# Attention output kept by channel and divided on GpSimd, in an FFN, attention, FFN block on one core

## The reference

```python
x = x + 0.5 * _L0_ffn_ref(_layernorm(x), w_gate, w_up, w_down)
x = x + _L0_attn_ref(_layernorm(x), Wq, Wk, Wv, Wo)
x = x + 0.5 * _L0_ffn_ref(_layernorm(x), w_gate, w_up, w_down)

def _L0_attn_ref(x, Wq, Wk, Wv, Wo):
    ...
    logits = jnp.where(causal_mask, neg, einsum('bhqd,bhkd->bhqk', q, k) * scale)
    out = einsum('bhqk,bhkd->bhqd', softmax(logits), v)
    return out.transpose(0, 2, 1, 3).reshape(B, T, D) @ Wo.T
```

## Time and profile before

| | us |
|---|---|
| median of 3 runs (2227.59 to 2228.46) | 2228.16 |
| the profiled execution | 2228.96 |
| its span, first to last instruction | 2227.2 |
| first feed-forward network, 40 to 460 | 420 |
| products for queries, keys, values, 460 to 690 | 230 |
| attention, 690 to about 1687 | 997 |
| output product, to about 1756 | 69 |
| second feed-forward network, to the end | 471 |

### The profile page before, as it was taken

How to read it: one execution, slowest core, us unless ns; L and a number is a source line. 1 busy time by engine, 2 the same in 40 slices (tenths; PEclk the granted TensorE clock), 3 DMA queues, 4 the chain that set the end, 5 groups by cost and what they waited for, 6 DMA issues and landing times. The chain is left out here.

```text
span 2227.2 us, 50129 instructions
## 1 busy us (share of the span) xinstructions
PE 2087.8 (94%) x13960; PEld 1374.4 (62%) x13960; DVE 1923.9 (86%) x4807; ACT 1313.3 (59%) x2413; POOL 1005.3 (45%) x1671
## 2 busy tenths in 40 slices
PE   4799999997998999999999999999998799999998
PEld 3688888886883333333333333333336788888887
DVE  6799999996987888888888888988863699999996
ACT  3455555543762777777677777777784344555553
POOL 4788888873654011111011111101110288888884
PEclk7899999998996999999999999999998899999998
DMA  6000000002689665545665546665403100000000
GB/s 210 1 1 0 0 0 0 0 1 71 229 234 181 76 78 72 72 65 70 77 78 66 71 63 77 78 78 67 55 12 122 35 16 19 19 19 19 19 19 25
DMA packets 163272, 133.33 MB, mean 60 GB/s; under 512 B 78432, under 2 KB 138208, under 8 KB 163040
## 3 DMA queue, kind: packets, MB, share of 16 engines
q1 hardware_dynamic: 163104, 131.25, 32.8%
HBM read 79.82 MB, written 51.38 MB: 59 GB/s over the span
## 5 line engine op out<-in xcount | busy, mean ns | idle before, releaser
L1413 POOL TENSOR_SCALAR_AFFINE_SELECT diag_scores<-diag_scores 128x256 f32<-128x256 f32 x256 | 104.1, 406 | 876.9 <-ACT diag_scores L1373 870.9
L1436 DVE CUSTOM_DVE_ANT_0 gu_ps<-gu_ps,mask_qk 128x256 f32<-128x256 f32 (+3 forms) x801 | 372.5, 501 | 33.6 <-PE gu_ps L1243 31.6
L1376 ACT ACTIVATE probs<-hT_ps 128x1024 f32<-128x1024 f32 (+3 forms) x352 | 280.4, 796 | 176.4 <-PE hT_ps L1264 112.8
L1243 PE MATMUL gu_ps<-k_stack,q_stack 96*128 96x512 bf16 (+3 forms) x1121 | 327.1, 331 | 9.9 <-DVE part_max L1436 7.4
L1283 PE MATMUL gu_ps<-probs,v_group 128*17 128x512 f32 (+3 forms) x3072 | 323.1, 493 | 0.7 <-ACT probs L1381 0.6
L713 PE MATMUL gu_ps<-wguT_hi,ffn_xT_hi 128*128 128x512 f32 (+1 forms) x768 | 313.1, 408 | 7.2 <-DVE ffn_xT_lo L589 5.1
L1376 ACT ACTIVATE probs<-av_ps 128x1024 f32<-128x1024 f32 (+3 forms) x352 | 282.1, 801 | 22.3 <-PE av_ps L1260 17.6
L713 PE MATMUL gu_ps<-wguT_hi,ffn_xT_lo 128*128 128x512 f32 (+1 forms) x768 | 290.9, 379 | 0.0
L713 PE MATMUL gu_ps<-wguT_lo,ffn_xT_hi 128*128 128x512 f32 (+1 forms) x768 | 290.7, 379 | 0.0
L691 ACT ACTIVATE ffn_z<-xs,ffn_shift,ffn_rstd 128x256 f32 (+1 forms) x128 | 77.1, 602 | 349.8 <-POOL ffn_shift L642 349.8
L1441 DVE TENSOR_REDUCE part_max<-gu_ps 128x1 f32<-128x512 f32 x320 | 208.3, 683 | 62.9 <-PE gu_ps L1243 62.9
(11 more groups left out here) (215 smaller groups left out, 5084.9 us busy)
## 6 DMA issues: line engine op xcount, KB each, us to landing
q_stack<-q_parts SPq DMA_DIRECT2D x192, 128.0 KB, 6.7
k_stack<-k_parts SPq DMA_DIRECT2D x192, 128.0 KB, 7.5
q_parts<-qkv_parts SPq DMA_DIRECT2D x32, 384.0 KB, 2.7
k_parts<-qkv_parts SPq DMA_DIRECT2D x32, 384.0 KB, 2.8
v_ones<-qkv_vst SPq DMA_DIRECT2D x16, 544.0 KB, 3.8
v_group<-v_ones SPq DMA_DIRECT2D x32, 272.0 KB, 10.6
xs<-in_L_attn_x SPq DMA_DIRECT2D x8, 1024.0 KB, 12.0
attn_rows<-ao SPq DMA_DIRECT2D x64, 128.0 KB, 5.4
```

The source lines that it names most:

```text
L1243: mm = T.matmul(out[:, e, :], qs[0:STACK, h0 + e, t * P:(t + 1) * P], ks[0:STACK, h0 + e, c * CHUNK:c * CHUNK + w], start=True, stop=True)
L1376: S.activation(probs[:, pair, i % 2, :, first:w], scores[pair][:, :, first:w], ACT.Exp, scale=DH ** -0.5).then_inc(s[pr], 1)
L1413: G.affine_select(out=block_of, in_=block_of, compare_op=ALU.is_ge, fill=MASKED, base=0, pattern=[[0, 2], [1, P]], channel_multiplier=-1). ...
L1436: last = V.tensor_tensor_reduce(out=ps[:, e * w:(e + 1) * w], in0=ps[:, e * w:(e + 1) * w], in1=mask_qk[:, CHUNK - w:CHUNK], scale=1.0, sc ...
```

## The change

The attention output stays as it leaves the accumulator, one row for each channel and one column for each position. ScalarE copies a half into its own place of `o_sb`. In the diff, `divide` and the `group` that calls it are GpSimd's, and the branch on `per == GROUP` stands in `reduce_unit`. VectorE takes the reciprocal of the whole copy, 128 rows by 512 columns, into `rl`, although only the four rows of sums are used. SP writes these four rows to DRAM, waits for the landing, and reads each back 16 times over into the rows of its head's channels (`turn_sums`). GpSimd multiplies `o_sb` by `rl` (`divide`), and SP stores four pieces by channel into `attn_cols` (`send_out`). TensorE's transposes of the output, VectorE's division and `ao` go. The output product loads 256 channels by 512 positions and needs no transposes.

A group has 10 steps instead of 12: three for half 0 and seven for half 1, of which two join two narrow pieces. GpSimd masks three times per pair of heads instead of four, once two blocks at a time. The two units that have all four heads in one bank (t = 0 and the second part of t = 4) are masked by one addition and reduced by one reduction instead of four instructions. There are 38 units. All 32 groups are written out on every engine.

```diff
-            STEPS = [(0, t) for t in range(4)] + [(1, t + 4 * d) for t in range(4) for d in range(2)]
+            STEPS = [[(0, 0)], [(0, 3), (0, 1)], [(0, 2)], [(1, 0)], [(1, 4)], [(1, 1)], [(1, 7), (1, 5)], [(1, 2)],
+                     [(1, 6)], [(1, 3)]]
+            HALF = 3
...
-            MAX_STEP = 7
+            MAX_STEP = 6
...
-                o_sb = sb(ctx, "o_sb", [P, CHUNK], F32)
-                rl = sb(ctx, "rl", [P, 4, GROUP], F32)
+                o_sb = sb(ctx, "o_sb", [P, 2, CHUNK], F32)
+                rl = sb(ctx, "rl", [P, CHUNK], F32)
...
                 def groups(eng, group):
-                    for g in range(GROUPS):
-                        group(0, g, False)
-                    with eng.Fori(1, BATCH - 1) as b:
+                    for b in range(BATCH):
                         for g in range(GROUPS):
-                            group(b, g, False)
-                    for g in range(GROUPS):
-                        group(BATCH - 1, g, True)
+                            group(b, g, b == BATCH - 1)
...
                         def send_out(b, g, j):
                             n2 = (b * GROUPS + g) * 2 + j
                             once(sp, "ao", n2, 1)
...
+                            for h in range(GROUP):
+                                ch = (g * GROUP + h) * DH
+                                sp.dma_start(attn_cols[ch:ch + DH, b * SEQ + j * CHUNK:b * SEQ + (j + 1) * CHUNK],
+                                             o_sb[h * VPAD:h * VPAD + DH, j, :]).then_inc(ao_stored[j], 16)
+                        def turn_sums(b, g, j):
+                            n2 = (b * GROUPS + g) * 2 + j
+                            once(sp, "rl", n2, 1)
+                            sp.dma_start(inverse[n2, :, :], rl[DH:P:VPAD, :]).then_inc(s["inverse"], 16)
+                            sp.wait_ge(s["inverse"], 16 * (n2 + 1))
+                            for h in range(GROUP):
+                                at = h * VPAD
+                                sp.dma_start(rl[at:at + DH, :], inverse[n2, h:h + 1, :].broadcast_to([DH, CHUNK])
+                                             ).then_inc(s["turned"], 16)
...
                                 fill(sp, *nxt)
                             if prev:
+                                turn_sums(*prev, 1)
                                 send_out(*prev, 1)
-                            send_out(b, g, 0)
+                            turn_sums(b, g, 0)
                             nxt = later(b, g, 1, last)
                             if nxt:
                                 send_max(*nxt)
+                            send_out(b, g, 0)
...
-                        def turn_out(b, g, j, ps):
-                            once(pe, "o_sb", (b * GROUPS + g) * 2, j + 1)
-                            for t in range(4):
-                                mm = T.transpose(ps[:, t * P:(t + 1) * P], o_sb[:, t * P:(t + 1) * P], ident[:])
-                            mm.then_inc(s["oT"], 1)
...
                         def copy_out(b, g, j):
...
+                            once(act, "pv", n * NS, (HALF, NS)[j])
+                            if n:
+                                act.wait_ge(ao_stored[j], n * GROUP * 16)
+                            S.copy(o_sb[:, j, :], o_ps[:, :]).then_inc(s["o_sb"], 1)
...
+                        def divide(b, g, j):
+                            n2 = (b * GROUPS + g) * 2 + j
+                            pool.wait_ge(s["turned"], 16 * GROUP * (n2 + 1))
+                            G.tensor_tensor(o_sb[:, j, :], o_sb[:, j, :], rl[:, :], ALU.mult).then_inc(s["ao"], 1)
...
                         def group(b, g, last):
+                            prev = before(b, g)
+                            if prev:
+                                divide(*prev, 1)
+                            causal(b, g, 0)
+                            causal(b, g, 1)
+                            divide(b, g, 0)
+                            causal(b, g, 2)
...
+                            if per == GROUP:
+                                out = ps[:, :].rearrange("p (h w) -> p h w", h=per)
+                                V.tensor_tensor(out, out, mask_qk[:, CHUNK - w:CHUNK].unsqueeze(1)
+                                                .broadcast_to([P, per, w]), ALU.add).then_inc(s["masked"], 1)
+                                once(dve, "masked", n * 2, t // 4 + 1)
+                                last = V.tensor_reduce(part_max[:, :, t, c], out, AX.X, ALU.max)
...
                         def one_over(b, g, j):
...
+                            n2 = (b * GROUPS + g) * 2 + j
+                            once(dve, "ao", n2, 0)
+                            once(dve, "o_sb", n2, 1)
+                            V.reciprocal(rl[:, :], o_sb[:, j, :]).then_inc(s["rl"], 1)
...
-                                halves = {2: (prev, 1), 6: ((b, g), 0)}.get(i)
+                                halves = {2: (prev, 1), HALF + 2: ((b, g), 0)}.get(i)
```

```diff
-                        sp.dma_start(attn_in[:, r, :, :], attn_rows[bass.ds(c * CHUNK, CHUNK), :]
-                                     .rearrange("(t p) c -> p t c", p=P)).then_inc(a_loaded[r], 16)
+                        sp.dma_start(attn_in[:, r, :, :], attn_cols[:, bass.ds(c * CHUNK, CHUNK)]
+                                     .rearrange("(k p) c -> p k c", p=P)).then_inc(a_loaded[r], 16)
...
-                            last = S.copy(aT[0][:, buf, k, :], aT_ps[buf][:, k, :])
+                            last = S.copy(aT[0][:, buf, k, :], attn_in[:, nr, k, :])
...
-                            last = V.tensor_tensor(aT[1][:, buf, k, :], aT_ps[buf][:, k, :],
+                            last = V.tensor_tensor(aT[1][:, buf, k, :], attn_in[:, (r + 1) % A_RING, k, :],
```

More of the change, by code:

```diff
@@ L380, in step @@
                 def step(c, r, turn):
[L381 to L389, removed]
                     if has(c):
@@ L774, in build @@
         att_sem = {n: sem(f"att_{n}") for n in
-                   ("cleared smax reduced mx mT m_hi m_lo m_stored scoresA scoresB probsA probsB diag taken causal pv "
-                    "o_sb oT rl ao filled").split()}
+                   ("cleared smax masked reduced mx mT m_hi m_lo m_stored scoresA scoresB probsA probsB diag taken causal pv "
+                    "o_sb rl inverse turned ao filled").split()}
         stack_loaded = [sem(f"stack_loaded{r}") for r in range(RING)]
@@ L1059, in attention, with columns, pieces @@
             NG = BATCH * GROUPS
-            STEPS = [(0, t) for t in range(4)] + [(1, t + 4 * d) for t in range(4) for d in range(2)]
+            STEPS = [[(0, 0)], [(0, 3), (0, 1)], [(0, 2)], [(1, 0)], [(1, 4)], [(1, 1)], [(1, 7), (1, 5)], [(1, 2)],
+                     [(1, 6)], [(1, 3)]]
             NS = len(STEPS)
-            DIAG = [i for i, (j, t) in enumerate(STEPS) if j and t >= 4 * j]
-            widths = [CHUNK - max(0, t - 4 * j) * P for j, t in STEPS]
-            WIDE_DIAG = [i for i in DIAG if widths[i] > P]
+            HALF = 3
+            def columns(j, t):
+                return CHUNK - max(0, t - 4 * j) * P
+            def pieces(i):
+                at = 0
+                for j, t in STEPS[i]:
+                    yield j, t, at, columns(j, t)
+                    at += columns(j, t)
+            widths = [sum(columns(j, t) for j, t in step) for step in STEPS]
+            on_diag = [sum(t >= 4 * j for j, t in step) for step in STEPS]
+            DIAG = [i for i in range(HALF, NS) if on_diag[i]]
             UNITS = []
@@ L1231, in bank_free @@
                                     return
-                                if kind == "turn_out" and (which[0] == 0 or before(b, g)):
-                                    once(pe, "ao", n * 2, 1 if which[0] == 0 else 0)
-                                    return
                                 e -= BANKS
@@ L1259, in score_head @@
                                 once(pe, pairs[pair][1], n * NS, i)
-                            mm = T.matmul(scores[pair][:, e, 0:widths[i]], ks[0:STACK_MAX, h, t * P:(t + 1) * P],
-                                          qs[0:STACK_MAX, h, (j + 1) * CHUNK - widths[i]:(j + 1) * CHUNK],
-                                          start=True, stop=True)
-                            if t >= 4 * j and i not in DIAG:
-                                mm = T.matmul(scores[pair][:, e, 0:P], ident_bf[:], mask_kq[:], start=False, stop=True,
-                                              skip_group_check=True)
+                            for j, t, at, w in pieces(i):
+                                mm = T.matmul(scores[pair][:, e, at:at + w], ks[0:STACK_MAX, h, t * P:(t + 1) * P],
+                                              qs[0:STACK_MAX, h, (j + 1) * CHUNK - w:(j + 1) * CHUNK],
+                                              start=at == 0, stop=True, skip_group_check=True)
+                            if on_diag[i] and i not in DIAG:
```

(6 more changed lines are left out.)

124 lines of the change are left out of this document (45 added, 79 removed).

## The result

The changed kernel takes 2539.91 us (median of four runs, 2538.55 to 2542.8) against 2228.31 for the kernel before, run beside it: 1.140 times as long, with an interval of 1.138 to 1.142. Predicted were 2570 us, between 2440 and 2700. The profiled execution took 2542.8 us, with a span of 2541.0.

The account below looks back on a forecast made before the run. TensorE was taken to bound the kernel, VectorE having 3.1 us a group to give. Groups 1 to 28 +349, last three +10, group 0 +2, restarts -20, tail +9.5, output product -9: +341, 2570 us, range 2440 to 2700.

Parts of the forecast that it names:

- The mechanism: Attention groups: sums wait behind the fill, delaying division, masks and second reciprocal; a group takes 42.0 us instead of 29.54.
- ScalarE's wait for the masks: Step (1, 4): masks behind GpSimd's late division hold ScalarE, the longest wait of the stage, near 9 us.
- The reciprocal: VectorE, twice a group: 128x512 takes 3.4 us by 6.3 ns a column, so 6.8 us a group.
- The prediction's group without a fill: Last attention groups, where the sums do not wait behind loads: about 33.8 us a group.
- the wait behind the fill: SP's queue in attention: the sums' write lands only at the fill's end, +19.35; adds 8.2 us a group.
- Earlier steps have the same work as now, so they hide nothing of it: Attention group before step (1, 4): the values' 9 us delay, +25.3 instead of +16.34, counts in full.
- The clock's 1.7 us: TensorE after its pause in each group: lower granted clock adds 1.7 us, bounds 0 and 4.5.
- The restarts: Attention loop: writing out the groups saves the loop's restarts, 20.3 us, bounds 0 to -20.3.
- the case in which it doesn't: Rival, SP's queue: write and reads land in 2 us despite the fill; 33.8 us a group, 2347 us, chance 0.12.
- the in-between case: Rival, SP's queue: only the write passes, reads land at the fill's end; 38.5 us a group, 2472 us, chance 0.07.
- Faster: Rival, attention: reciprocal takes 0.68 us and the round trip ends before step (1, 4) needs GpSimd; 2181 us, chance 0.03.
- the written-out code is fetched too slowly: Rival, written-out attention groups: slow code fetching, so the 20 us do not come; 2590 us, chance 0.02 (no change).

Follow-up runs that it names:

- the small fill: Changed kernel with each fill load from group 4 on fetching only a small part of its tile: 2399.2 us.
- the run with the copy: Changed kernel with VectorE's reciprocal of 128x512 replaced by a copy of the same size: 2482.2 us.
- a queue edit: Changed kernel with SP issuing the fill behind the previous half 1's write and four reads of the sums instead of ahead of them: 2493.3 us.
- the last run: Changed kernel with one narrow round trip a group for both halves, its steps moved earlier: 2191.8 us, 0.983 times the kernel before.

## Why the prediction held, and which of its terms were off

*The mechanism* went as written, but for what hides what. Forecast and measured, from the group's first scores: sums landed and reads issued, +19.35 and +19.55; last read +20.9 and +20.9, landed +22.9 and +22.7; division done +24.0 and +24.0; second reciprocal +24.0 to +27.4 and +24.03 to +27.4; values of step (1, 4) +25.3 and +25.34; next group +42.0 and +40.95. GpSimd's product was priced at 1.06 us and takes 1.266, which the slightly earlier landing paid for. Two waits were forecast too long: TensorE was to be without work from about +17.5 to +25.3 and stands still for 4.44 us, and ScalarE's wait for the masks was to be near 9 us and is 6.49. The reason for both follows below.

*The reciprocal* was forecast at 3.4 us from three narrower rows and takes 3.348: (3.348 - 0.752) / 416 = 6.2 ns a column beyond 96 columns. The Trainium skill ("VectorE: DVE Perf Modes", "First, the fixed hardware budget") has a repeat count of eight for the divide; eight cycles of that page's 0.96 GHz are 8.3 ns, an estimate. The measured row disagrees with it and decides for 6.2.

*The sum of the causes was nearly right and its split was wrong.* The prediction's group without a fill was 33.8 us, and the wait behind the fill was to add 8.2. Measured are these periods of the new form: 28.4 with neither (30.5 where 13 small loads are still issued), 36.8 in group 29 and 35.8 with the small fill with the reciprocals alone, 39.7 with the fill alone, 41.0 with both. Against 28.4, the reciprocals alone cost 8.4 us and the fill 11.3; together they cost 12.6, not 19.7. The step that had this wrong is "Earlier steps have the same work as now, so they hide nothing of it". They don't end where they did. Timeline of TensorE in group 29, which begins at 1907.75, and the last of these rows again in group 29 of the run with the copy, which begins at 1868.22:

```profile
1918.87 0.34 PE L1253 MATMUL xd_ps<-k_stack,q_stack 96*128 96x384 bf16 x1 [1.73 <-DVE part_max L1461]
...
1928.61 1.05 PE L1294 MATMUL gu_ps<-probs,v_group 128*17 128x512 f32 x8
...
1883.66 1.05 PE L1294 MATMUL gu_ps<-probs,v_group 128*17 128x512 f32 x8
```

Behind the first reciprocal TensorE waits 1.73 us for a free bank. The wait ends 11.1 us into the group, and from about 12 on the clock is at 0.51 for 7 us (group 13 does the same, the stretch from 1264.60). The values of step (1, 4), the row at 1928.61, come at +20.86 instead of +16.34, although the division is done by +16.6 and TensorE waits for no mask. With the copy they come at +15.44, so the first reciprocal makes them 5.4 us late; against the kernel before it is 4.5. In group 13 TensorE is through with its other work at about the same point, +20.9, and stands still for 4.44 us until the values at +25.34, whose time the sums set. So the fill adds 4.5 us there and not 9. TensorE's waits in the changed kernel show the pair of pauses, of which the working had only the second:

```profile
PE gu_ps L1294 <- ACT probs L1380: 150.9, 30, 6.5
PE xd_ps L1253 <- DVE part_max L1461: 51.8, 30, 1.7
PE gu_ps L1253 <- DVE part_max L1456: 35.2, 35, 2.2
```

From the values of step (1, 4) to the next group it is 15.9 us in group 29 and 15.6 in group 13, against 13.2 before and 13.0 with the copy; the forecast for group 13 was 16.7. The prediction's 33.8 us had neither the first pause nor a term for the clock. The clock alone is large enough for the 3 us by which it was too low: TensorE's busy time in group 29 is 32.72 us at 0.86 and 27.53 at 1.00 with the copy, 5.2 us apart. How much of these a group without the low clock would save isn't measured. That 42.0 came close to 40.95 all the same is owed to the queue, which sets the time of the values whatever the first reciprocal does.

*The term by term account* of the span, 2541.0 - 2227.2 = +313.8:

- Groups 1 to 28: 28 x 11.46 = +321 (forecast +349). The clock's 1.7 us and the rest behind the values were 1.0 too much. The prediction put the smaller work of the new form at nothing; group 29 of the run with the copy takes 28.4 us instead of 29.5, which would account for it, but no run shows it in a group with a fill.
- Groups 29 to 31: 36.8, 31.9 and 24.2 against 29.5, 27.1 and 22.7, +13.5 (forecast +10).
- Up to group 0's copy of half 1: +5.1 (forecast +2).
- The restarts: -20.3, as forecast, and -20.6 in the same 24 groups when they go alone.
- From the last copy to VectorE's last instruction: 540.0 us before and 534.7 after, -5.3 (forecast +0.5). In it, the rows that the output product loads are there 16.60 us after the last copy (2003.55 to 2020.15) instead of 6.88 (1684.48 to 1691.36), +9.7 where +9.5 was forecast. From there to its last multiplication it is 51.4 us instead of 64.4, -13.0 where -9 was forecast; a chunk takes 2.87 us (2027.01 to 2029.88) as forecast (2.9) instead of 3.71. The rest, -2, lies in the feed-forward behind it and wasn't looked into.

*The rivals.* The queue did hold the write back (9.0 us against 1.7), so neither the case in which it doesn't nor the in-between case came. Had it not, the time would not have been 2347 us either: with the small fill it is 2399. The Trainium skill ("DMA: Bandwidth & Descriptors", "Queues, rings and completion order") allows a later DMA on few engines to complete before an earlier one on all. In group 13 the four-row write got ahead by 0.2 us only: the reads that wait for it go out at 1272.07, and the fill's last load, issued at 1261.04, lands 11.2 us later, at 1272.24. Whether the order of the queue or the busy DMA engines held it isn't separated. "Faster" fell with the 3.35 us, above its threshold of 1.8; the run with the copy shows that its second condition, a round trip that ends in time, would have failed too. That the written-out code is fetched too slowly fell with the run that has this part alone (2206.9 us).

## What to carry to other kernels

When two causes each hold up the same step, the gains of taking away one and the other don't add up to the gain of both: here the copy gave 58 us and the small fill 141, and the two together 311 of the 312. Look up in the trace of each single edit what ends the wait now: a queue edit can simply hand the wait to the next transfer behind the bulk load (47 us here). On an operation that costs time per column, count columns: the 4096 sums of two halves as 128x32 cost 0.34 us where each half as 128x512 costs 3.35. The trip through DRAM that this needs cost at most 0.8 us a group (29.2 against 28.4) once its transfers stood between the loads and not behind them.

## What the runs showed of the hardware

- In each of the groups 1 to 30 of the changed kernel TensorE stood still for 1.73 us behind the first reciprocal, and about 1 us after it went on the clock was at its lower level. In 10 of them (13 and 29 among these) it read 0.51 on average over the next 6.9 us, in the other 20 it read 0.75. The rows before had shown it only after 3.3 us and more. In a group where TensorE waits less it stays at 1.00 (28.61 us with 27.63 busy, group 13 of the last run).
- GpSimd's product of two full 128x512 tensors takes 1.266 us, a fifth above the 1.06 of the line through its products with 256 and 704 columns. No run tells why.
- SP issued the 128 KB loads of a fill 0.46 us apart (13 issues from 1255.49 to 1261.04 in group 13) and small loads at the same pace; 13 small loads delayed what stood behind them by 2.1 us.
- Written-out groups ran without a pause: 28 groups of 29.53 us on average with the kernel before, least 29.48, most 29.77.
